# Block-diagonal products of a graph network on TensorE: two 128x128 stages recut into 64x64 products of two chunks on the four quarters of the array

## The reference, cut to what matters

```
def _L2_gnn_ref(features, A, W1, b1, W2, b2):
    ...
    _, U = jnp.linalg.eigh(L_norm)
    agg = jnp.einsum('mn,bnd->bmd', U.T, features)
    h = jax.nn.relu(agg @ W1 + b1)
    out = h @ W2 + b2
    return jnp.einsum('nm,bmd->bnd', U, out)
...
def _slconv(x, adj, S, W):
    support = jnp.einsum('bnf,fh->bnh', x, W)
    weighting = adj * S
    return jnp.einsum('nm,bmh->bnh', weighting, support)
h = jax.nn.relu(_slconv(x, adj, S, W1))
h = jax.nn.relu(_slconv(h, adj, S, W2))
return _slconv(h, adj, S, W3)
...
x = x + _L2_gnn_ref(h, adj, ...)
h = jnp.maximum(_layernorm(x, axis=-1), 0.0)
x = x + _L3_gnn_ref(h, adj, adj, ...)
```

## Time and profile before

| | before |
|---|---|
| median of 3 runs | 971.79 us (970.81 to 972.17) |
| the profiled execution, own time | 972.66 us |
| its span, first to last instruction | 970.9 us |
| mean granted TensorE clock | 0.961 |
| busy: PE, DVE, ACT, POOL | 88%, 57%, 53%, 33% |

### The profile page before, as it was taken

How to read it: one execution, slowest core, us unless ns; L and a number is a source line. 1 busy time by engine, 2 the same in 40 slices (tenths; PEclk the granted TensorE clock), 3 DMA queues, 4 the chain that set the end, 5 groups by cost and what they waited for, 6 DMA issues and landing times.

```text
span 970.9 us, 12291 instructions
## 1 busy us (share of the span) xinstructions
PE 852.6 (88%) x3723; PEld 565.7 (58%) x3723; DVE 557.1 (57%) x2996; ACT 517.1 (53%) x958; POOL 316.6 (33%) x376
## 2 busy tenths in 40 slices
PE   2677767599899988988878988988999999999998
PEld 1344433364468646774456834766658758848846
DVE  5899867769778896796999545337005104304101
ACT  0466547356755746557645555675463463544521
POOL 1233111246555654556645556203002202202000
PEclk9999979889999999999989889998999999999999
DMA  8000000000000000000000000000000000100101
GB/s 342 0 1 1 1 0 1 1 1 1 0 1 1 1 1 1 1 1 1 0 1 0 1 1 0 1 1 1 1 0 35 11 0 1 44 0 1 44 1 44
DMA packets 2962, 13.27 MB, mean 14 GB/s; under 512 B 464, under 2 KB 464, under 8 KB 2640
## 3 DMA queue, kind: packets, MB, share of 16 engines
q1 hardware_dynamic: 2896, 12.48, 3.2%
HBM read 8.28 MB, written 4.19 MB: 13 GB/s over the span
## 4 chain that ended last, share of the span: by engine, by line
PE 54%; DVE 16%; ACT 4%; POOL 1%; issue 1%; ACTq 0%; DVEq 0%
PE PS L452 53%; DVE Fq L1467 1%; POOL BIG L994 1%; DVE seg L1468 1%; ACT T L869 1%; DVE PS L1361 1%; ACT BIG L903 1%; DVE PS L1363 1%; DVE Z L1368 1%; DVE Z L1365 1%; DVE stats L1643 1%; DVE X L1868 1%; ACT T L813 1%; DVE counts L1406 0%; PE PS L631 0%
## 5 line engine op out<-in xcount | busy, mean ns | idle before, releaser
L452 PE MATMUL PS<-BIG,wts 128*128 128x512 f32 (+2 forms) x952 | 341.8, 501 | 6.1 <-POOL BIG L994 5.0
L994 POOL TENSOR_TENSOR BIG<-BIG 128x256 f32<-128x256 f32 (+2 forms) x220 | 210.5, 966 | 154.5 <-ACT BIG L903 82.7
L452 PEld LDWEIGHTS PS<-BIG,wts 128*128 128x128 f32 x952 | 177.6, 193 | 127.6 <-issue 94.9
L903 ACT ACTIVATE BIG<-PS,lbias 128x256 f32<-128x256 f32 (+2 forms) x312 | 163.2, 560 | 115.7 <-PE PS L452 113.9
L452 PE MATMUL PS<-H,wts 128*128 128x256 f32 (+2 forms) x312 | 112.0, 488 | 12.4 <-ACT BIG L903 9.4
L805 ACT ACTIVATE BIG<-PS 128x1024 f32<-128x1024 f32 x64 | 65.5, 1024 | 88.5 <-PE PS L452 88.5
L1868 DVE TENSOR_TENSOR X<-X,PS 128x512 f32<-128x512 f32 x64 | 43.4, 682 | 115.0 <-PE PS L452 87.1
L805 ACT ACTIVATE T<-PS 128x512 f32<-128x512 f32 x96 | 55.9, 594 | 90.9 <-PE PS L452 90.6
L452 PE MATMUL PS<-T,wts 128*128 128x512 f32 x192 | 102.4, 655 | 2.0 <-ACT T L805 1.7
L971 POOL TENSOR_SCALAR rstd<-mv 128x4 f32<-128x4 f32 x48 | 11.0, 230 | 265.9 <-DVE mv L1671 265.9
L813 ACT ACTIVATE T<-X,shift,rstd 128x128 f32<-128x128 f32 x192 | 78.4, 481 | 34.6 <-DVE shift L1680 34.6
(11 more groups left out here) (318 smaller groups left out, 1237.5 us busy)
## 6 DMA issues: line engine op xcount, KB each, us to landing
X<-x_in SPq DMA_DIRECT2D x1, 4096.0 KB, 12.5
out<-X SPq DMA_DIRECT2D x16, 256.0 KB, 2.0
wts<-w_in SPq DMA_DIRECT2D x1, 3542.0 KB, 21.2
cst<-cst_in SPq DMA_DIRECT2D x1, 419.0 KB, 3.4
AA<-adj_in SPq DMA_DIRECT2D x2, 16.0 KB, 1.9
```

The source lines that it names most:

```text
L452: return nc.tensor.matmul(o, l, r, start=start, stop=stop)
L903: nc.scalar.activation(LB[:, q, {"i": I_, "g": G_, "f": F_, "o": O_}[g], 0:n], PS[:, 3 * q + rank[q] % 3, 0:n], ACT.Tanh if g == "g" else ...
L994: nc.gpsimd.tensor_tensor(out, a, b, op).then_inc(pool_set[q], 1)
```

## The change

`back` and `mix3` no longer multiply one chunk by the 128x128 block-diagonal matrix. They take two chunks k and k + 1 together and issue four products with 64x64 weights, each on another quarter of the array: graph g of chunk k from partitions g to partitions g (the diagonal quarters), then graph g of chunk k + 1 from partitions g to partitions 1 - g (the other two). That exchanges the two graphs of a tile in odd chunks. So that it comes out right, the step that stands an odd number of exchanges ahead uses a crossed matrix with its blocks off the diagonal: `agg` uses `crossed_U` and `mix1` uses `crossed_S` in odd chunks. Both waits of the two chunks now stand ahead of the pair. Two new 128x128 matrices are made: crossed_S with two copies from BDST at the start, crossed_U with a memset and two copies at the end of the eigenvector computation.

```diff
+        crossed_S = sb("crossed_S", [P, P])
+        crossed_U = sb("crossed_U", [P, P])
...
+            def quarters(k, weights, columns, out_bank):
+                for odd in range(2):
+                    for g in range(2):
+                        rows = slice(g * NODES, (g + 1) * NODES)
+                        to = slice((g ^ odd) * NODES, ((g ^ odd) + 1) * NODES)
+                        j = mm(out_bank(k + odd)[to, :], weights[rows, rows], T1[rows, k + odd, columns])
+                    j.then_inc(pe_done[k + odd], 1)
...
             def last_products(i):
...
-                for k in range(NK):
-                    pe.wait_ge(act_done[k], D_ACT.at(i, "s3"))
-                    mm(banks(k)[:, 1, :], BDST[:, :], T1[:, k, CH:2 * CH]).then_inc(pe_done[k], 1)
+                for k in range(0, NK, 2):
+                    for c in (k, k + 1):
+                        pe.wait_ge(act_done[c], D_ACT.at(i, "s3"))
+                    quarters(k, BDST, slice(CH, 2 * CH), odd_bank)
...
-                    tiles(bank(k), k, T0[:, k, :], BDU[:, :])
+                    tiles(bank(k), k, T0[:, k, :], (crossed_U if k % 2 else BDU)[:, :])
...
-                for k in range(NK):
-                    pe.wait_ge(dve_done[k], D_DVE.at(i, "o"))
-                    mm(bank(k), BDUT[:, :], T1[:, k, 0:CH]).then_inc(pe_done[k], 1)
+                for k in range(0, NK, 2):
+                    for c in (k, k + 1):
+                        pe.wait_ge(dve_done[c], D_DVE.at(i, "o"))
+                    quarters(k, BDUT, slice(0, CH), bank)
...
-                    tiles(bank(k), k, T0[:, k, :], BDST[:, :])
+                    tiles(bank(k), k, T0[:, k, :], (crossed_S if k % 2 else BDST)[:, :])
...
+                step(v.memset(crossed_U[:, :], 0.0))
...
+                    step(v.tensor_copy(crossed_U[h, (1 - b) * NODES:(2 - b) * NODES], eb(2)[h, n64]))
...
                     step(v.tensor_scalar(RB1[:, :], PS[:, 1, 0:P], W("bg1"), None, ALU.mult))
+                    step(v.tensor_copy(crossed_S[:, 0:NODES], BDST[:, NODES:P]))
+                    step(v.tensor_copy(crossed_S[:, NODES:P], BDST[:, 0:NODES]))
```

More of the change, by code:

```diff
@@ L1937, in _ @@
                 add(ITER - 1, k, banks(k)[:, 1, :], D_PE.at(ITER - 1, "mix3"))
-PREP = {"BDA": 1, "BDAT": 2, "hat_rows": 11, "lap_rows": 18, "S": 24, "biases": 30, "diagonals": 32, "bound": 45,
-        "ways": 63, "V": 104, "VT": 106, "U": 108, "AU": 111, "ritz": 116, "I+E": 129, "all": 135}
+PREP = {"BDA": 1, "BDAT": 2, "hat_rows": 11, "lap_rows": 18, "S": 24, "biases": 32, "diagonals": 34, "bound": 47,
+        "ways": 65, "V": 106, "VT": 108, "U": 110, "AU": 113, "ritz": 118, "I+E": 131, "all": 140}
 def kernel(x, adj, **w):
```

## The result

The changed kernel takes 964.25 us in the median of 5 runs (961.53 to 965.62); the kernel before 971.79 (968.21 to 972.23). The ratio is 0.9928 with a 95% interval of 0.9904 to 0.9952: 7 us faster, between 4.7 and 9.3. The prediction said 978.0 us and slower. It was wrong in direction; its first rival, all four quarters together at 965.9 us, had the mechanism right. The clock is not the cause: the granted clock is 0.961 in before's profile and 0.962 here.

A forecast was written before the change was run, and what follows sets the result against it. PE was taken to bound the last part. Six inner runs +4.6 us, iteration 0's back +0.57, the last mix3 +0.57 and the copies +0.45 made +6.2 us on the median 971.79: 978.0 us, range 963.5 to 980.

The forecast's parts named there:

- first rival: Runs of back and mix3: all four quarters stream together, 2.39 us a run against 3.44; 965.9 us in all; chance 36%.
- What bounds the kernel: Last part, from 670.42 us: PE is the bound, so a microsecond taken from it comes off the time, with two exceptions.
- what is held behind it is quarter B's first matmul: Runs of back and mix3: quarter A's waiting second matmul blocks quarter B; nine steps, 4.21 us a run, +0.77 each.
- The price of a run: Six inner runs with all four quarters together: 2.39 us against 3.44, -1.05 each, -6.3 in all.
- the ramp: Start of a run with all quarters together: D1 starts six small loads behind A1, 6 x 0.055 = 0.33 us.
- The change of mode: Around each run: switching PE into quarter mode and back costs 0.34 us; entering alone 0.14 us.
- Iteration 0: Back of iteration 0, where PE idles behind it: chunk 0 ready later, +0.57 us in the forecast, +0.25 with all quarters together.
- the last run: Mix3 of iteration 3, at the end: +0.57 us in the forecast, -0.25 with all quarters together, adds 0.69 us each.
- The copies: Two DVE copies for crossed_S in front of NI at the start: 0.22 us each, +0.45 us.
- The pair waits: Waits for two chunks ahead of each pair in back and mix3: cost nothing.
- 979.8 us: Whole kernel by the forecast if each mode change cost another 0.2 us.
- the queue in order: The forecast case for runs of back and mix3: in-order queue, only one overlap, 978.0 us, own range 975 to 980; chance 42%.

The follow-up runs named there:

- e6: Changed kernel with a run's eight products ordered by quarter, behind waits for all four chunks; 972.35 us, ratio to the kernel before 1.0017.
- e7: Changed kernel with all eight products of a run on one quarter, the second graph's left out; 998.45 us, ratio to the kernel before 1.0282.
- e2: Kernel before with each chunk's product in back and mix3 cut into two 64x64 products on the diagonal quarters, no exchange; 972.18 us, ratio 1.0017.
- e8: Changed kernel with back of iteration 0 and mix3 of iteration 3 put back to the whole array; 963.84 us, ratio to the kernel before 0.9930.
- e11: Changed kernel with mix2 also cut into quarters, 64x64 stationary parts and 64 moving columns; 957.65 us, ratio to the kernel before 0.9857.
- e10: Kernel before with five short memsets more in VectorE's program, where VectorE is idle; 973.32 us, ratio 1.0017.
- e1: Changed kernel with the crossed matrices still made but every product put back to the whole array; 972.31 us, ratio to the kernel before 1.0012.
- e9: Changed kernel with the two crossed matrices made on GpSimd instead of VectorE; 962.76 us, ratio to the kernel before 0.9910.
- e5: Changed kernel with the four products of a pair in the order A, C, B, D instead of A, B, C, D; 963.44 us, ratio to the kernel before 0.9931.

## Why the prediction was wrong

- **What bounds the kernel** held: what was taken from PE's six inner runs came off the time, and the two runs at the ends gave +0.15 and -0.73.
- **The step that failed** is "what is held behind it is quarter B's first matmul". It made a run nine steps and 4.21 us long, +0.77 each; measured are 2.13 us, -1.31. From the steady state of the whole array I read that a matmul whose quarter still streams is held at the head of the queue, which is true or not visible there, since every matmul in those rows needs the same quarter. The rows could not show what happens to a matmul for another one. The windows of the changed kernel show four first matmuls together and four second ones after them; e6 shows the same with three waiting. e7 shows that within one quarter they do follow each other at 0.43 us. So a matmul waits for its own quarter only, and program order does not hold between quarters. "TensorE: Matmul & The Clock Gate" of the Trainium skill, What overlaps and what doesn't, says strictly in program order; the measurement differs, and it decides. I had taken the rule for support of a step that the trace left open.
- **The price of a run** in the rival was -1.05 us; it measured -7.88/6 = -1.31 (in the trace, -1.28 for a run of back and -1.36 for one of mix3). The term that was off is the ramp: 0.33 us for six loads, 0.055 apart as in the earlier trace rows. Those rows are loads into the same quarter. Into different quarters, eight loads take 0.21 us, one alone 0.13, so they start 0.01 apart and there is no ramp.
- **The change of mode** at 0.34 us for both ways was right: 3.44 - 1.31 = 2.13 us a run, less 4 x 0.43 is 0.41, some 0.05 of it the spread of the starts and the pair wait. e2 confirms it from another side, with 2.07/6 = 0.34.
- **Iteration 0** was put at +0.25 (rival) and measured +0.15; **the last run** at -0.25 and measured -0.73 up to the last add, since the first add comes 1.12 us after the run's start where it was 1.07, only 0.05 later and not 0.25, and since four adds in a row take 2.48 us and not 4 x 0.69.
- **The copies** were put at 0.45 and measured 0.51; NI itself moves by 0.4 us between executions of kernels with the same code ahead of it (31.28 us in e8, 31.69 in e11), so this is no closer than that. **Missing from the sum** was the tail, +1.3 us, 1.1 of it for five more VectorE instructions (e10), which no term covered.
- **The rival's number** is partly luck. Its 965.9 us is 1.7 above the measured 964.25 because errors of opposite sign meet: six runs 1.6 us too dear and the end 0.5, against a tail of 1.3 us that it left out.
- **The pair waits** at nothing were nearly right, up to 0.09 us for a run of back; e6 shows that waiting for all four chunks would have cost 0.84 to 0.94 us a run.
- **A slip in a bound**: 979.8 us for 0.2 us more at each mode change does not come out of the working; eight runs give 978.0 + 1.6 = 979.6.

The chances, 42% for the queue in order and 36% for the quarters together, were near even for a question that the trace did not decide. The range was drawn to 963.5 and 980, and the median lies in it.

## What to carry to other kernels

A block-diagonal weight matrix wastes half the array, and cutting it into the two diagonal blocks wins nothing (e2). The gain comes from the two off-diagonal quarters, if the neighbouring matrix can be crossed so that the exchange costs nothing. A step of small products gains too (e11), where each 128-column load with its matmul took 0.11 us; that this is due to the shorter loads and not to the quarters was not separated. Going into the mode and back costs 0.34 to 0.41 us here, so it pays for runs of several products. Where a step hands over an instruction every 0.007 us, pauses of 1.0 to 1.3 us came with it in three iterations of four. Before ruling out an overlap from a steady state, ask whether any row has two instructions that need different parts of the engine; if none has, the question is open and a small probe is worth more than the argument.

## What was not expected of the hardware

- Matmuls of different quarters pass each other: a quarter's second matmul starts behind the first matmul of a quarter that comes five places later in the program, and three may wait without holding up others (e6).
- Five more VectorE instructions, all of them ahead of 575 us, lengthened the end of the span from 2.5 to 3.5 us (e1, e10); with the same matrices made on GpSimd it was 2.7 (e9).
- Identical code reached the last part at 646.6 (e5) to 653.0 us (e11) in different executions. Below 0.5% a stretch of the trace that repeats to 0.1 us (317.20, 317.21, 317.19) tells more than the medians of a dozen runs.
- 0.007 us for one matmul or load handed to the array in e11, and a pause of 1.03 us in three iterations of four, after 418, 454 and 490 of them, each behind a 16 KB packet on an instruction queue.
